# Value sums of the masked keys: from token sums on VectorE and one product with Wv, in place of three products with V

## The chip, the cores and the metric

One core of one Trainium2 chip. The metric is the device time of one execution in microseconds (us), the median of several runs.

## The reference

Eight batches of 512 tokens of width 128. Each token is layer-normalized to `xn`; an attention head and a mixture of 8 experts (the top two of them by gate) both read `xn`, and both results are added to `x`. What matters here is how the attention masks: the scores are multiplied by the mask, so that a masked key has the score 0, and it still takes part in the softmax.

```python
attn = jnp.einsum('bqe,bke->bqk', q, k)
mask = jnp.tril(jnp.ones((T, T), dtype=attn.dtype))
attn = attn * mask
attn = jax.nn.softmax(attn / jnp.sqrt(jnp.asarray(T, attn.dtype)), axis=-1)
return jnp.einsum('bqk,bke->bqe', attn, v)
```

So a row of queries needs, beside the weighted values of the keys it may see, the plain sum of the values of all masked keys, times exp(-max). With T = 512 in NT = 4 tiles of 128 tokens, the keys of all tiles after the query's own are masked for the whole tile; the kernel takes the sum of their values once for each tile of queries.

## The kernel before

All engines run their own lists of instructions, ordered by hand, with semaphores between them. A batch passes through these steps:

- `normal_stats`, `normal_finish` (VectorE), `normal_rstd` (GpSimd), `normalize` (ScalarE) give `xn`; `transpose_x` (TensorE, into a PSUM bank, group X), `x_hi` (ScalarE) and `x_lo` (VectorE) give the transposed tokens as a high and a low part, `xT_hi` and `xT_lo`. A product is three matmuls of these (`three`): high by high, high by low, low by high.
- `wide(b, k, t)` multiplies tile t by a group of the stacked weights: C is Wv, expert 7 and the gates (264 columns), A four experts (512), B three (384). `project_u` (group U) gives `uT` for the scores, with `u_hi` and `u_lo`.
- `c_copy` (ScalarE) copies C, so V too, to SBUF (`c_s`); `scale_experts` (ScalarE) and `mix_b` (VectorE) take A and B out of PSUM; `sum_experts` (GpSimd) adds.
- `scores`, `mask_scores`, `negate_max`, `softmax_exp`, `transpose_probs`, `probs_copy`, `attend` are the attention. The chain for the gates is `gate_max`, `gate_drop`, `gate_below` (VectorE), `gate_exp` (ScalarE), `gate_sum`, `gate_rec`, `gate_out` (VectorE).
- `value_sums` (group SV) multiplies V by a matrix of ones and zeros, `suffix`, one f32 matmul for each of the tiles 1 to 3, so that the rows of query tile t get the sum of the values of all later tiles. `sv_high` (ScalarE) and `sv_rows` (VectorE) put them into the right side of the product `bias`, whose left side comes from `bias_rows` (GpSimd), `transpose_rows` (group DT) and `rows_copy`. `bias` closes the sum in the bank `attb`; `finish_tile` (VectorE) waits for it and writes the output.

The PSUM banks of the groups X, U, SV, DT, A, B and C form a ring of four in a fixed order, and a group waits until the one four places earlier was read. The steady order, for pass n of the loop (n from 1 to 6; + is batch n+1, - is batch n-1), is

```python
GROUPS = "C3 B2- B3- A3- SV DT- A0 B0 X+ A1 B1 C0+ U+ C1+ C2+ A2".split()
...
if prev == "X":
    pe.wait_ge(S["xl_ready"], b + 1)
elif prev in ("U", "SV", "DT"):
    pe.wait_ge(S[{"U": "ul_ready", "SV": "sv_rows_ready", "DT": "dt_ready"}[prev]], b + 1)
```

So U+ waits for what `x_lo` leaves, C2+ for the last `mix_b` of B1 (`mix_ready`), and the next C3 for `u_lo`. TensorE's list has, from C3 on, in pass n: C3(n), B2(n-1), B3(n-1), `attend(n-1, 1)`, `scores(n, 0)`, `transpose_probs(n-1, 2)`, A3(n-1), `transpose_probs(n-1, 3)`, `value_sums(n)`, `attend(n-1, 2)`, `scores(n, 1)`, `transpose_rows(n-1)`, `attend(n-1, 3)`, `bias(n-1)`. VectorE's list, after `x_lo`, has `mask_scores(n-1, 2)`, `mix_b(n-1, 1, 0..2)` with some `normal_stats` between, `u_lo(n)`, `mask_scores(n-1, 3)`, `mix_b(n-1, 2, 0)`, which waits for B2, and then the gates. ScalarE has `softmax_exp(n-1, 3)`, `gate_exp(n)`, `probs_copy(n-1, 2)`, `scale_experts(n-1, 3)`, `probs_copy(n-1, 3)`.

Of the kernel before, what the change touches and what calls it, by code (L numbers as in the profile page):

```python
# [37 lines left out]
ALU = mybir.AluOpType  # L38
# [43 lines left out]
def build(nc, x, w_attention, w_stacked, be, shapes, out):  # L82
# [10 lines left out]
    with ExitStack() as ctx:  # L93
        def sb(name, shape, dt=F32):
            return ctx.enter_context(nc.sbuf_tensor(name, shape, dt))
# [4 lines left out]
        def sem(name):  # L100
# [9 lines left out]
        warm = sb("warm", [P, 1])  # L110
        ident = sb("ident", [P, P])
        causal = sb("causal", [P, NT * P])
        suffix = sb("suffix", [P, NT, P])
        half = sb("half", [P, NT])
        ones = sb("ones", [P, NT, 2, E])

# [38 lines left out]
            veps_ready nmean_ready rstd_ready stats_ready gate_ready nmx_ready tot_ready rinv_ready fin_done  # L155
            rows_ready ffn_ready y7_ready sv_rows_ready stored0 stored_last ones_ready xn0_dve_ready
            wc_ready wcl_ready xt_late_done xh_late_ready rstd0_ready wa_ready wb_ready wla_ready wlb_ready
            ah_ready beh_ready stored1 dve_chain pool_chain ident_ready consts_ready low_ready"""
        S = {n: sem(n) for n in names.split()}

        block = ctx.enter_context(nc.Block())
# [30 lines left out]
        def bank(g, b):  # L192
            return ring[place[g, b] % RING]
# [29 lines left out]
        def _(pe):  # L223
            def ring_free(g, b):

                n = place[g, b] - RING
                if n < 0:
                    return
                prev, b = sequence[n]
                if prev == "X":  # L230
                    pe.wait_ge(S["xl_ready"], b + 1)
                elif prev in ("U", "SV", "DT"):
                    pe.wait_ge(S[{"U": "ul_ready", "SV": "sv_rows_ready", "DT": "dt_ready"}[prev]], b + 1)
                else:
                    pe.wait_ge(S[{"C": "c_used", "A": "a_used", "B": "mix_ready"}[prev[0]]], NT * b + int(prev[1]) + 1)
# [25 lines left out]
            def scores(b, t):  # L261

                if t == 0:
                    pe.wait_ge(S["uh_ready"], b + 1)
                if b * NT + t >= SCORE_BANKS:

                    pe.wait_ge(S["pt_ready"], b * NT + t + 1 - SCORE_BANKS)
                r, n = slice(t * P, (t + 1) * P), (t + 1) * P
                three(score_bank(b, t)[:, 0:n], uT_hi[:, b % 2, r], uT_lo[:, b % 2, r], xT_hi[:, b % 2, 0:n],
                      xT_lo[:, b % 2, 0:n], (S["ul_ready"], b + 1) if t == 0 else None).then_inc(S["scores_done"], 1)  # L270
# [44 lines left out]
            def value_sums(b):  # L315

                ring_free("SV", b)
                pe.wait_ge(S["c_used"], b * NT + NT)
                for m in range(1, NT):
                    last = nc.tensor.matmul(bank("SV", b)[:, 0:P], suffix[:, m, :], c_s[:, b % 2, m, 0:P],  # L320
                                            start=(m == 1), stop=(m == NT - 1))
                last.then_inc(S["sv_done"], 1)

            def transpose_rows(b):

# [132 lines left out]
        def _(dve):  # L458
# [159 lines left out]
            def x_lo(b):  # L618

                dve.wait_ge(S["xh_ready"], b + 1)  # L620
                split_lo(xT_lo[:, b % 2, :], bank("X", b)[:], xT_hi[:, b % 2, :], S["xl_ready"])

            def weights_lo(b):

                dve.wait_ge(S["wa_ready"], 1)
                split_lo(w_lo[:, a_cols], w_f[:, a_cols], w_hi[:, a_cols], S["wla_ready"])
# [28 lines left out]
            dve.wait_ge(S["xh_ready"], 1)  # L655
            split_lo(xT_lo[:, 0, early], bank("X", 0)[:, early], xT_hi[:, 0, early], S["xl_ready"])

            normal_stats(1, 0)
            normal_stats(1, 1)
            normal_stats(1, 2)  # L660
            normal_stats(1, 3)
            bias_rhs(0)
# [17 lines left out]
            mix_b(0, 0, 1)  # L680
            mix_b(0, 0, 2)
            x_lo(1)

            for n in range(1, B - 1):
                mask_scores(n - 1, 2)
                mix_b(n - 1, 1, 0)
                normal_stats(n + 1, 0)
                mix_b(n - 1, 1, 1)
                negate_max(n - 1, 2)
                mix_b(n - 1, 1, 2)  # L690
                normal_stats(n + 1, 1)
                normal_stats(n + 1, 2)
                u_lo(n)
                mask_scores(n - 1, 3)
                mix_b(n - 1, 2, 0)
                negate_max(n - 1, 3)
                mix_b(n - 1, 2, 1)
                normal_stats(n + 1, 3)
                gate_max(n)
                mix_b(n - 1, 3, 0)  # L700
                gate_drop(n)
                gate_below(n)
                softmax_sum(n - 1)
                mix_b(n - 1, 2, 2)
                softmax_tot(n - 1)
                normal_finish(n + 1)
                mix_b(n - 1, 3, 1)
                gate_sum(n)
                mix_b(n - 1, 3, 2)
                mask_scores(n, 0)  # L710
                softmax_rec(n - 1)
                negate_max(n, 0)
                gate_rec(n)
                mask_scores(n, 1)
                negate_max(n, 1)
                finish_tile(n - 1, 0)
                gate_out(n)
                sv_rows(n, 0)
                sv_rows(n, 1)
                sv_rows(n, 2)  # L720
                mix_b(n, 0, 0)
                finish_tile(n - 1, 1)
                mix_b(n, 0, 1)
                finish_tile(n - 1, 2)
                mix_b(n, 0, 2)
                finish_tile(n - 1, 3)
                x_lo(n + 1)

            mix_b(B - 2, 1, 0)
            mix_b(B - 2, 1, 1)  # L730
            mask_scores(B - 2, 2)
            mix_b(B - 2, 1, 2)
            negate_max(B - 2, 2)
# [55 lines left out]
        def _(act):  # L789
# [15 lines left out]
            def c_copy(b, t):  # L805

                act.wait_ge(S["wide_done"], wide_count("C", b, t))
                if t == 0 and b > 1:

                    act.wait_ge(S["pv_done"], (b - 1) * NT)  # L810
                    act.wait_ge(S["sv_done"], b - 1)
                    act.wait_ge(S["y7_ready"], b - 1)
                nc.scalar.copy(c_s[:, b % 2, t, 0:COLS["C"]], bank(f"C{t}", b)[:, 0:COLS["C"]]).then_inc(S["c_used"], 1)

# [165 lines left out]
        def _(pool):  # L980
# [69 lines left out]
            for t in range(1, NT):  # L1050
# [2 lines left out]
            nc.gpsimd.affine_select(out=ident[:], in_=ident[:], compare_op=ALU.not_equal, fill=1.0, base=0,  # L1053
                                    pattern=[[-1, P]], channel_multiplier=1).then_inc(S["ident_ready"], 1)
            nc.gpsimd.memset(top8[:, :, E:E + 2], LOW)
            nc.gpsimd.memset(c_s[:, :, :, COLS["C"]:COLS["C"] + 2], LOW).then_inc(S["low_ready"], 1)
            nc.gpsimd.memset(em[:], 0.0)
            full = chain.mark(nc.gpsimd.memset(causal[:], 1.0))
            cleared = chain.mark(nc.gpsimd.memset(suffix[:], 0.0))
            chain.need(full)  # L1060
            nc.gpsimd.affine_select(out=causal[:, (NT - 1) * P:], in_=causal[:, (NT - 1) * P:], compare_op=ALU.is_ge, fill=0.0, base=0,
                                    pattern=[[-1, P]], channel_multiplier=1)
            chain.need(cleared)

            for m in range(1, NT):
                v = suffix[:, m, :].rearrange("p (t r) -> p t r", r=ROWS)
                last = nc.gpsimd.memset(v[:, 0:m, 0:G_ROW], 1.0)
            chain.step(last)
            normal_rstd(0)
            pool.wait_ge(S["wb_ready"], 1)  # L1070
            nc.gpsimd.tensor_tensor(w_lo[:, b_cols], w_f[:, b_cols], w_hi[:, b_cols].bitcast(F32), ALU.subtract
# [61 lines left out]
```

## Time and profile before

| | |
|---|---|
| median of 3 runs | 132.51 us (130.95 to 132.6) |
| the profiled execution, its own time | 132.71 us |
| its span, from the first to the last instruction | 130.7 us |
| TensorE busy | 121.3 us, 93% |
| VectorE busy | 102.1 us, 78% |
| ScalarE busy | 101.4 us, 78% |
| GpSimd busy | 96.2 us, 74% |

The 1.9 us between the span of the profiled execution and its time lie around the instructions. TensorE's matmuls are pipelined and their ends are modelled, so that its busy time covers short waits too. An instruction on the other engines may start before the record of the one before it has ended. A pass of the steady loop takes 13.90 us.

### The profile page before, as it was taken

The page shows a single profiled execution, that of the slowest core. Times are in us where ns is not written, and L with a number is a line of the kernel's source. Part 1 is how long each engine was busy: PE and PEld are TensorE (multiplying, and loading weights), DVE is VectorE, ACT ScalarE, POOL GpSimd, SP SyncE. Part 2 cuts the span into 40 slices and gives each one's busy share as a digit, 9 for nine tenths or more (in the row PEclk, how much of TensorE's full clock was granted, in tenths as well). Part 3 has the DMA queues.
Part 4 walks back from the last instruction along what each step waited for, and adds up shares of the span by engine and source line. Part 5 has one row for each costly group of instructions (what it writes and reads, how often), then busy time and mean ns, then how long its engine had stood idle before and what let it go on. Part 6 is the DMA issues. An engine that isn't in the chain of part 4 may idle for free.

```text
span 130.7 us, 3014 instructions
## 1 busy us (share of the span) xinstructions
PE 121.3 (93%) x766; PEld 109.1 (83%) x766; DVE 102.1 (78%) x507; ACT 101.4 (78%) x341; POOL 96.2 (74%) x216
## 2 busy tenths in 40 slices
PE   4839999999999999999999999999999999999870
PEld 4717878998989989999899999999899899888650
DVE  0477789797988799697969796979877985967822
ACT  2145699979986999789996999699869999656850
POOL 7080228669995998689967997799859986788881
PEclk9999999999999999999999999999999999999999
DMA  2996000000020002000200020000200020002002
GB/s 65 362 295 164 0 0 8 0 3 3 10 70 5 3 0 80 0 0 3 82 3 3 0 78 10 0 0 7 78 5 0 0 80 0 0 5 83 3 0 80
DMA packets 8929, 5.18 MB, mean 40 GB/s; under 512 B 328, under 2 KB 8784, under 8 KB 8912
## 3 DMA queue, kind: packets, MB, share of 16 engines
q1 hardware_dynamic: 8608, 4.79, 12.5%
q10 hardware_dynamic: 304, 0.20, 0.5%
q8 instruction: 6, 0.10, 0.3%
q14 instruction: 11, 0.09, 0.2%
HBM read 2.89 MB, written 2.10 MB: 38 GB/s over the span
## 4 chain that ended last, share of the span: by engine, by line
PE 83%; DVE 7%; DMA 3%; POOL 2%; ACT 1%; issue 1%; POOLq 0%
PE ring L239 13%; PE ring L240 13%; PE ring L243 13%; PE attb L293 12%; PE score L277 6%; PE ring L320 4%; PE score L243 4%; PE score L240 4%; PE score L239 3%; DMA x_all<-in_x_dram 3%; PE ring L302 2%; PE ring L310 2%; PE ring L313 2%; PE ring L311 2%; DVE xn L648 2%; PE ring L328 1%
## 5 line engine op out<-in xcount | busy, mean ns | idle before, releaser
L829 ACT ACTIVATE ysc<-ring,gate 128x128 f32<-128x128 f32 x128 | 36.4, 372 | 3.4 <-DVE gate L528 1.5
L239 PE MATMUL ring<-w_hi,xT_hi 128*128 128x264 f32 (+2 forms) x96 | 35.2, 367 | 0.6 <-DVE mix L543 0.4
L240 PE MATMUL ring<-w_lo,xT_hi 128*128 128x264 f32 (+2 forms) x96 | 33.0, 344 | 0.0
L243 PE MATMUL ring<-w_hi,xT_lo 128*128 128x264 f32 (+2 forms) x96 | 32.9, 343 | 0.0
L1010 POOL TENSOR_TENSOR ysc<-ysc 128x256 f32<-128x256 f32 x32 | 23.5, 734 | 7.3 <-ACT ysc L829 7.3
L293 PE MATMUL attb<-c_s,probT 128*128 128x128 f32 x160 | 23.3, 278 | 0.0
L543 DVE SCALAR_TENSOR_TENSOR mix<-ring,gate,mix 128x128 f32<-128x128 f32 x64 | 22.0, 344 | 0.2
L239 PEld LDWEIGHTS ring<-w_hi,xT_hi 128*128 128x128 f32 x96 | 18.7, 194 | 3.3 <-DVE mix L543 0.6
L293 PEld LDWEIGHTS attb<-c_s,probT 128*128 128x128 f32 x160 | 20.8, 191 | 0.4
L240 PEld LDWEIGHTS ring<-w_lo,xT_hi 128*128 128x128 f32 x96 | 18.6, 194 | 1.6
L243 PEld LDWEIGHTS ring<-w_hi,xT_lo 128*128 128x128 f32 x96 | 18.5, 193 | 1.4
L1017 POOL TENSOR_TENSOR ffn<-ysc,mix 128x128 f32<-128x128 f32 x32 | 14.6, 457 | 6.5 <-DVE tot L582 4.3
L840 ACT ACTIVATE prob<-score,nmx 128x128 f32<-128x128 f32 (+3 forms) x32 | 17.4, 542 | 0.6 <-DVE nmx L567 0.6
L543 DVE SCALAR_TENSOR_TENSOR mix<-ring,gate,x_all 128x128 f32<-128x128 f32 x32 | 11.0, 345 | 7.9 <-PE ring L243 7.7
L597 DVE SCALAR_TENSOR_TENSOR o_s<-attb,rinv,ffn 128x128 f32<-128x128 f32 x32 | 10.8, 344 | 8.0 <-PE attb L334 7.9
L1013 POOL TENSOR_TENSOR ysc<-ysc,y 128x128 f32<-128x128 f32 x32 | 14.7, 461 | 2.5
L1011 POOL TENSOR_TENSOR ysc<-ysc 128x128 f32<-128x128 f32 x32 | 14.7, 459 | 2.5
L560 DVE CUSTOM_DVE_ANT_0 score<-score,causal 128x128 f32<-128x128 f32 (+3 forms) x32 | 15.7, 490 | 0.1
L990 POOL TENSOR_TENSOR rstd<-veps,half 128x4 f32<-128x4 f32 x8 | 8.1, 1014 | 9.5 <-DVE veps L475 5.9
L277 PE MATMUL score<-ident,prob 128*128 128x128 f32 x80 | 14.2, 276 | 0.2 <-ACT prob L840 0.2
L855 ACT COPY probT<-score 128x128 f32<-128x128 f32 (+3 forms) x32 | 13.8, 430 | 0.4 <-PE score L277 0.3
L801 ACT ACTIVATE xn<-x_all,nmr,rstd 128x128 f32<-128x128 f32 x29 | 12.0, 483 | 1.6 <-POOL nmr L998 1.6
(99 smaller groups left out, 248.9 us busy)
## 6 DMA issues: line engine op xcount, KB each, us to landing
x_all<-in_x_dram SPq DMA_DIRECT2D x8, 256.0 KB, 5.9
out_dram<-o_s SPq DMA_DIRECT2D x7, 256.0 KB, 2.3
w_f<-in_w_stacked_dram SPq DMA_DIRECT2D x1, 580.0 KB, 5.2
out_dram<-o_s SPq DMA_DIRECT2D x1, 192.0 KB, 2.1
wqk_s<-in_w_attention_dram ACTq DMA_DIRECT2D x1, 128.0 KB, 3.7
shapes_s<-in_shapes_dram ACTq DMA_DIRECT2D x1, 64.5 KB
out_dram<-o_s SPq DMA_DIRECT2D x1, 64.0 KB, 1.8
be_s<-in_be_dram ACTq DMA_DIRECT2D x1, 4.0 KB
```

Of the source, the lines that this page charges most:

```text
L239: nc.tensor.matmul(dst, hi, w_h, start=True, stop=False)
L240: nc.tensor.matmul(dst, hi, w_l, start=False, stop=False)
L243: return nc.tensor.matmul(dst, lo, w_h, start=False, stop=True)
L277: last = nc.tensor.transpose(score_bank(b, t)[:, c], prob[:, t, c], ident[:])
L293: last = nc.tensor.matmul(attb[:, t * P:(t + 1) * P], probT[:, b % 2, t, j * P:(j + 1) * P], c_s[:, b % 2, j, 0:P], start=(t == 0), stop=F ...
L543: ins = nc.vector.scalar_tensor_tensor(mix[:, t, i, :], bank(f"B{t}", b)[:, i * P:(i + 1) * P], gate[:, b % 2, t, 4 + i:5 + i], before, AL ...
L560: cnt["maxed", b, t] = chain.mark(nc.vector.tensor_tensor_reduce(score_bank(b, t)[:, 0:n], score_bank(b, t)[:, 0:n], causal[:, (NT - 1 - t ...
L829: last = nc.scalar.mul(ysc[:, t, e, :], bank(f"A{t}", b)[:, e * P:(e + 1) * P], gate[:, b % 2, t, e:e + 1])
L840: nc.scalar.activation(prob[:, t, 0:n], score_bank(b, t)[:, 0:n], ACT.Exp, bias=nmx[:, b % 2, t:t + 1], scale=1.0, accum_out=rs[:, b % 2, ...
L1010: chain.step(nc.gpsimd.tensor_tensor(y[:, 0:2, :], y[:, 0:2, :], y[:, 2:4, :], ALU.add))
L1011: chain.step(nc.gpsimd.tensor_tensor(y[:, 0, :], y[:, 0, :], y[:, 1, :], ALU.add))
L1013: chain.step(nc.gpsimd.tensor_tensor(y[:, 0, :], y[:, 0, :], y7[:, b % 2, t, :], ALU.add))
```

## The change

The sum of the values of a tile's tokens is the sum of its normalized tokens times Wv. VectorE now sums the tokens of tiles 1 to 3 along the free dimension, straight from the PSUM bank of the transposed tokens (`token_sums`, after `x_lo`), adds neighbours (`token_sums_pairs`) and adds the third and spreads the result to the columns of each query tile's rows (`token_sums_later`). One f32 matmul of `x_sums` with the f32 weights (`w_f`, whose first 128 columns are Wv) takes the place of the three. The bank X is now free only once the token sums are taken (`xsum_ready`), and `value_sums` waits for `sums_ready` instead of the copies of V. For batch 0, where tiles 2 and 3 lie in a score bank, there are two reductions, and `scores(0, 2)` waits for them. The constant `suffix` and its memsets go, and two small memsets come.

```diff
@@ ring_free
                 if prev == "X":
-                    pe.wait_ge(S["xl_ready"], b + 1)
+                    pe.wait_ge(S["xsum_ready"], b + 1)
@@ scores
+                if b == 0 and t == 2:
+                    pe.wait_ge(S["xsum_ready"], 1)
@@ value_sums
-                pe.wait_ge(S["c_used"], b * NT + NT)
-                for m in range(1, NT):
-                    last = nc.tensor.matmul(bank("SV", b)[:, 0:P], suffix[:, m, :], c_s[:, b % 2, m, 0:P],
-                                            start=(m == 1), stop=(m == NT - 1))
-                last.then_inc(S["sv_done"], 1)
+                pe.wait_ge(S["sums_ready"], b + 1)
+                if b == 0:
+                    pe.wait_ge(S["w_moe"], 16)
+                nc.tensor.matmul(bank("SV", b)[:, 0:P], x_sums[:].rearrange("p t r -> p (t r)"), w_f[:, 0:P], start=True,
+                                 stop=True).then_inc(S["sv_done"], 1)
@@ new functions on VectorE
+            def token_sums(b):
+                tiles = bank("X", b)[:, P:NT * P].rearrange("p (t k) -> p t k", k=P)
+                nc.vector.tensor_reduce(xs[:, 0:NT - 1], tiles, AX_X, ALU.add).then_inc(S["xsum_ready"], 1)
+            def token_sums_pairs(b):
+                dve.wait_ge(S["xsum_ready"], b + 1)
+                nc.vector.tensor_tensor(xs2[:], xs[:, 0:NT - 1], xs[:, 1:NT], ALU.add).then_inc(S["xs2_ready"], 1)
+            def token_sums_later(b):
+                dve.wait_ge(S["xs2_ready"], b + 1)
+                if b > 0:
+                    dve.wait_ge(S["sv_done"], b)
+                nc.vector.tensor_tensor(x_sums[:, 0:NT - 1, 0:G_ROW], xs2[:].unsqueeze(2).to_broadcast([P, NT - 1, G_ROW]),
+                                        xs[:, 2:NT + 1].unsqueeze(2).to_broadcast([P, NT - 1, G_ROW]), ALU.add
+                                        ).then_inc(S["sums_ready"], 1)
@@ VectorE's list, batch 0
+            dve.wait_ge(S["low_ready"], 1)
+            nc.vector.tensor_reduce(xs[:, 1:NT - 1], late_x[:, early].rearrange("p (t k) -> p t k", k=P), AX_X, ALU.add)
+            nc.vector.tensor_reduce(xs[:, 0:1], bank("X", 0)[:, P:2 * P], AX_X, ALU.add).then_inc(S["xsum_ready"], 1)
             normal_stats(1, 0)
+            token_sums_pairs(0)
             normal_stats(1, 1)
+            token_sums_later(0)
@@ the loop (in the last pass and for batch 1 in the same way)
             for n in range(1, B - 1):
                 mask_scores(n - 1, 2)
+                token_sums_pairs(n)
                 mix_b(n - 1, 1, 0)
                 normal_stats(n + 1, 0)
                 mix_b(n - 1, 1, 1)
+                token_sums_later(n)
                 negate_max(n - 1, 2)
...
                 x_lo(n + 1)
+                token_sums(n + 1)
@@ c_copy on ScalarE
-                    act.wait_ge(S["sv_done"], b - 1)
@@ constants on GpSimd
+            nc.gpsimd.memset(xs[:], 0.0)
+            nc.gpsimd.memset(x_sums[:], 0.0)
...
-            cleared = chain.mark(nc.gpsimd.memset(suffix[:], 0.0))
...
-            for m in range(1, NT):
-                v = suffix[:, m, :].rearrange("p (t r) -> p t r", r=ROWS)
-                last = nc.gpsimd.memset(v[:, 0:m, 0:G_ROW], 1.0)
-            chain.step(last)
```

## Rows read from the trace of the kernel before

**Rows 1.** Windows, one steady pass: PE, PEld, DVE, ACT, POOL busy (count), clock, DMA, GB/s.

```profile
59.30:73.20 13.90, 13.90 (x95) 12.79 (x94) 11.94 (x62) 12.21 (x43) 11.52 (x25) 1.00 0.07 21
```

**Rows 2.** The chain that ended last, 60 to 74 us: start, us, what.

```profile
70.30 0.67 PE ring L320 x6
...
71.99 0.22 PE ring L328
72.22 0.98 PE attb L293 x8
```

**Rows 3.** Timeline of the TensorE weight loads: start, length, [idle before].

```profile
63.58 0.19 PEld L310 LDWEIGHTS ring<-xT_hi,a_hi 128*128 128x128 f32 x1
...
65.35 0.19 PEld L239 LDWEIGHTS ring<-w_hi,xT_hi 128*128 128x128 f32 x1
...
66.29 0.19 PEld L239 LDWEIGHTS ring<-w_hi,xT_hi 128*128 128x128 f32 x1
...
71.89 0.14 PEld L328 LDWEIGHTS ring<-ident,lhs_rows 128*128 128x128 f32 x1
72.04 0.97 PEld L293 LDWEIGHTS attb<-c_s,probT 128*128 128x128 f32 x8
```

**Rows 4.** Timeline of the TensorE matmuls, same pass.

```profile
67.22 0.34 PE L243 MATMUL ring<-w_hi,xT_lo 128*128 128x384 f32 x1
...
72.06 1.15 PE L293 MATMUL attb<-c_s,probT 128*128 128x128 f32 x8
```

**Rows 5.** Timeline of ScalarE, same pass.

```profile
69.87 0.23 ACT L819 ACTIVATE gexp<-below 128x32 f32<-128x32 f32 x1 [1.01 <-DVE below L507]
...
71.38 0.61 ACT L855 COPY probT<-score 128x512 f32<-128x512 f32 x1
```

**Rows 6.** Timeline of GpSimd, same pass.

```profile
71.52 0.26 POOL L1041 TENSOR_TENSOR lhs_rows<-gate_tot,lhs_rows 128x32 fp32r<-128x32 f32 x1
```

**Rows 7.** Timeline of VectorE, same pass.

```profile
62.58 0.68 DVE L480 TENSOR_TENSOR xT_lo<-ring,xT_hi 128x512 fp32r<-128x512 f32 x1
63.18 0.55 DVE L560 CUSTOM_DVE_ANT_0 score<-score,causal 128x384 f32<-128x384 f32 x1
...
64.48 0.35 DVE L543 SCALAR_TENSOR_TENSOR mix<-ring,gate,mix 128x128 f32<-128x128 f32 x1
...
65.23 0.69 DVE L480 TENSOR_TENSOR uT_lo<-ring,uT_hi 128x512 fp32r<-128x512 f32 x1
...
67.60 0.35 DVE L543 SCALAR_TENSOR_TENSOR mix<-ring,gate,x_all 128x128 f32<-128x128 f32 x1 [1.02 <-PE ring L243]
...
69.65 0.19 DVE L507 TENSOR_TENSOR below<-kept,top 128x32 f32<-128x32 f32 x1
...
70.10 0.15 DVE L582 TENSOR_TENSOR tot<-tot,rs 128x4 f32<-128x4 f32 x1
```

**Rows 8.** Timeline of all engines in the last pass.

```profile
113.56 0.26 POOL L1041 TENSOR_TENSOR lhs_rows<-gate_tot,lhs_rows 128x32 fp32r<-128x32 f32 x1
...
113.94 0.14 PEld L328 LDWEIGHTS ring<-ident,lhs_rows 128*128 128x128 f32 x1 [0.24 <-issue]
```

**Rows 9.** Timeline of all engines, start of the kernel.

```profile
15.71 0.91 PE L320 MATMUL ring<-c_s,suffix 128*128 128x128 f32 x6 [0.28 <-ACT c_s L813]
```

**Rows 10.** Groups of instructions by form, whole span.

```profile
L320 PE MATMUL ring<-c_s,suffix 128*128 128x128 f32 x48 | 6.8, 279 | 0.3 <-ACT c_s L813 0.3
...
L480 DVE TENSOR_TENSOR uT_lo<-ring,uT_hi 128x512 fp32r<-128x512 f32 x8 | 5.5, 691 | 1.3 <-ACT uT_hi L859 1.2
...
L560 DVE CUSTOM_DVE_ANT_0 score<-score,causal 128x384 f32<-128x384 f32 x8 | 4.4, 555 | 0.0
...
L513 DVE TENSOR_REDUCE gsum<-gexp 128x4 f32<-128x32 f32 x8 | 1.4, 172 | 0.0
```

**Rows 11.** Timeline of VectorE in the first, shorter pass.

```profile
23.14 0.48 DVE L465 BATCH_NORM_STATS2 stats<-x_all 128x6 f32<-128x128 f32 x2
```

**Rows 12.** Timeline of the weight loads in the first pass.

```profile
24.45 0.19 PEld L239 LDWEIGHTS ring<-w_hi,xT_hi 128*128 128x128 f32 x1 [0.20 <-DVE uT_lo L480]
```

More of the change, by code:

```diff
@@ L112, in build @@
         causal = sb("causal", [P, NT * P])
-        suffix = sb("suffix", [P, NT, P])
+        xs = sb("xs", [P, NT + 1])
+        xs2 = sb("xs2", [P, NT - 1])
+        x_sums = sb("x_sums", [P, NT, ROWS])
         half = sb("half", [P, NT])
@@ L157, in build @@
             wc_ready wcl_ready xt_late_done xh_late_ready rstd0_ready wa_ready wb_ready wla_ready wlb_ready
-            ah_ready beh_ready stored1 dve_chain pool_chain ident_ready consts_ready low_ready"""
+            ah_ready beh_ready xsum_ready xs2_ready sums_ready stored1 dve_chain pool_chain ident_ready consts_ready low_ready"""
         S = {n: sem(n) for n in names.split()}
@@ L682, in _ @@
             x_lo(1)
+            token_sums(1)
             for n in range(1, B - 1):
                 mask_scores(n - 1, 2)
+                token_sums_pairs(n)
                 mix_b(n - 1, 1, 0)
@@ L727, in _ @@
                 x_lo(n + 1)
+                token_sums(n + 1)
             mix_b(B - 2, 1, 0)
+            token_sums_pairs(B - 1)
             mix_b(B - 2, 1, 1)
+            token_sums_later(B - 1)
             mask_scores(B - 2, 2)
@@ L1062, in _ @@
                                     pattern=[[-1, P]], channel_multiplier=1)
-            chain.need(cleared)
-            for m in range(1, NT):
-                v = suffix[:, m, :].rearrange("p (t r) -> p t r", r=ROWS)
-                last = nc.gpsimd.memset(v[:, 0:m, 0:G_ROW], 1.0)
-            chain.step(last)
             normal_rstd(0)
```

## The prediction

> **What bounds the kernel now.** I read the windows first. In a pass of the steady loop TensorE is busy for all of the 13.90 us, at the full clock, with VectorE, ScalarE and GpSimd near 12 us each [rows 1]. That says "TensorE is the bound", and by it every matmul taken away is a gain. But the ends of matmuls are modelled, so I next read the chain that ended last piece by piece. The six records of the three value products take 0.67 us, 0.112 each [rows 2]. The transpose of the rows is one such record and takes 0.22, and the eight records of `attend(n-1, 3)` take 0.98 where 8 x 0.112 is 0.89 [rows 2]. So about 0.2 us of waiting is hidden there. The third view, the timelines, says for what: GpSimd ends the last of the rows at 71.78 and TensorE loads for their transpose at 71.89; ScalarE ends `probs_copy(n-1, 3)` at 71.99 and TensorE loads for `attend(n-1, 3)` at 72.04, and its matmul starts at 72.06 [rows 3 to 6]. TensorE takes both as soon as they are there.
>
> Where do these come from? Backwards on the timelines: `probs_copy(n-1, 3)` lies in ScalarE's unbroken run from `gate_exp`, which starts at 69.87 after 1.01 us of waiting for `gate_below` [rows 5]. `gate_below` ends at 69.84 on VectorE, in an unbroken run that starts at 67.60 with `mix_b(n-1, 2, 0)` after 1.02 us of waiting for B2 [rows 7], whose last matmul ends at 67.22 + 0.34 = 67.56 [rows 4]. GpSimd's part hangs on `softmax_tot`, 70.10, in the same run of VectorE [rows 7]. So from the end of B2 to `attend(n-1, 3)` there is a path of 4.5 us over VectorE and ScalarE (and one over GpSimd) that is as long as what TensorE does meanwhile, waits included. The three value products lie inside this stretch. The rest of the pass, 9.4 us from `attend(n-1, 3)` to the next B2, is TensorE's own work.
>
> **The change part by part.**
>
> *The two products less.* Four of the six records go: 4 x 0.112 = 0.45 us a batch [rows 2], 3.6 us for eight. The remaining one has the same shape (128 x 128, f32), so it keeps 0.22 us. In the steady pass TensorE now comes to the transpose of the rows and to `attend(n-1, 3)` 0.45 us earlier, and both inputs come no earlier, because VectorE's run still starts at the end of B2, ScalarE's with it, and nothing in either is shortened. What TensorE saves it waits. I take 0 for the gain; the bound on the other side is 0.45 less what TensorE waits already, were the two inputs not what it waits for. In the last pass the same rows end on GpSimd at 113.56 + 0.26 = 113.82, and TensorE, which the profile has idle there for 0.24 us, loads at 113.94 [rows 8]: no gain either. At the start the value product waits 0.28 us for the copies of V [rows 9], a wait that goes, but the next work of TensorE there is the transpose of the probabilities, which hangs on VectorE's mask and ScalarE's exponential: 0.
>
> *The reduction.* 384 elements of f32 from PSUM. The trace has no such reduction. The nearest rows are the mask of 384 columns from PSUM, 555 ns, and the reduction of 32 elements, 172 ns; the 512-column split is 691 ns, so an element costs (691 - 555) / 128 = 1.06 ns [rows 10]. 172 + 352 x 1.06 = 545 ns, and the mask's 555 is the other reading. I take 0.55. One instruction starts some 0.08 us before the record ahead of it ends (`x_lo` starts at 62.58, is 0.68 long, and the mask starts at 63.18, [rows 7]), so VectorE's list moves by 0.47 us. From both sides: 0.28 (two elements a step), 1.0 (two steps an element).
>
> *The two small sums.* By `softmax_tot` (0.15) and `gate_below` (0.19) [rows 7], less the overlap of 0.08: 0.07 + 0.11 = 0.18 us. A wait that needs an instruction of its own could double this. Altogether VectorE's list is 0.65 us later from there on, at most 1.2.
>
> *Who waits for that.* VectorE has 1.02 us to spare before `mix_b(n-1, 2, 0)`, so the run of the gates starts as before. Three steps before it are nearer.
> (a) U+ now waits for the reduction instead of `x_lo`. The reduction starts at 63.18 and ends at 63.73; with the 0.05 us from a producer's end to the load (as 71.99 to 72.04, [rows 3, 5]) U loads at 63.78 and not at 63.58 [rows 3]: 0.20 us. Queued behind U are `scores(n, 3)`, C1+, C2+, A2, C3 and B2, all of the path.
> (b) C2+ waits for the third `mix_b` of B1, which ends at 64.48 + 0.35 = 64.83 [rows 7], then at 65.48; its load is at 65.35 [rows 3], or 65.55 after (a): nothing more.
> (c) C3 waits for `u_lo`, 65.23 to 65.92 [rows 7], then to about 66.5; its load is at 66.29 [rows 3], or 66.49 after (a): about nothing more.
> (a), (b) and (c) overlap, so I count one. Loads run ahead of their matmuls, and a few hundredths of a late one are absorbed: 0.17 us for a pass. It lies in the stretch that is TensorE's own work, outside the path over VectorE, so it adds to the pass in full. It happens for batches 2 to 7: 6 x 0.17 = 1.0 us.
> In the first pass VectorE is closer: C3 already waits 0.20 us for `u_lo` there, its load is at 24.45 [rows 12], and VectorE comes to `u_lo` at 23.14 + 0.48 - 0.08 = 23.54 [rows 11]. With 0.65 more it starts at 24.19 and ends at 24.88, and C3 loads at 24.93: 0.45 us (0.48 less the few hundredths).
> Before that, batch 0's reductions go ahead of statistics that have time until `u_lo(0)`: 0, and at most 0.1.
>
> *GpSimd and ScalarE.* The memsets of `suffix` go and two smaller ones come, long before GpSimd's first real work: 0. The wait taken from `c_copy` was on a product long done: 0.
>
> **The sum.** 0 for the products, + 6 x 0.17 + 0.45 = +1.5 us. On the profiled execution's 132.71 us that is 134.2; the median of before is 0.2 lower, so 134.0 us.
>
> [...] The trace shows a reduction of 32 elements no slower than `gate_below` of 32 (172 against about 190 ns, [rows 7, 10]). [...]
>
> **The rivals.**
>
> *TensorE is the bound after all* (the windows are right, and the waits that I read are the model's): 8 x 0.45 = 3.6 us go, and the wait at U costs up to 1.5: 128.9 to 130.4 us. For it: 100% busy, and VectorE's 1.02 us idle. Against it: 0.05 us between ScalarE's end and TensorE's load in the same pass [rows 3, 5], and the rows that take 0.22 instead of 0.11. A half case is that ScalarE's and GpSimd's ends give 0.1 to 0.2 us in a pass: 132.5 to 133.4, within 2%. Chance 0.13 for the full one.
>
> *The reduction is slow.* Of this kernel's mechanisms the one that ends on the other side: U+ waits for it alone, and every 0.1 us over 0.55 adds 0.1 in each of seven batches, 0.7 us in all. The time is above 135.2 (2%) when it takes over about 0.70 us; at 1.0 us it is 134.0 + 7 x 0.45 = 137.2. By then VectorE is also 1.1 us later and uses up its 1.02 us before B2. For it: unseen size and PSUM source, two added waits; in the first pass there is no slack at all. Against it: every row of VectorE from PSUM shows one element in 1.06 ns. Chance 0.17, mostly at 135.3 to 136.5.
>
> *The change doesn't do what it says*: if the one product with `w_f` took as long as the three, nothing in my sum would change, since I count no gain. It has no case of its own.
>
> **How the numbers follow.** My forecast, 132.3 to 135.2, has 0.70: two hundredths of a us in (a) are 0.1 us in the time, and the half case of the first rival lies in it. Faster by over 2% is below 129.9: 0.12. Slower by over 2%: 0.18. 2% is about what a measurement of this kernel tells from no change (its three runs of before lie 1.2% apart). The range leaves out the full first rival and the far end of the second: 131.2 to 136.0.
>
> **What would show each step.** The value product as two records of about 0.11 us in place of six. The reduction near 0.55 us, right after `x_lo`. TensorE's load for U some 0.05 us behind the reduction's end, with the wait put down to VectorE. TensorE waiting 0.4 to 0.6 us in a pass before the transpose of the rows or `attend(n-1, 2)` and `attend(n-1, 3)`, for ScalarE and GpSimd. VectorE's wait for B2 down from 1.02 to about 0.5 us. A steady pass of 14.05 to 14.1 us. I am wrong if the pass is 13.6 or less (the path over VectorE is not what TensorE meets), or if U doesn't wait.

## The result, and the profile after

The changed kernel takes 135.88 us (median of 4 runs) where the kernel before takes 132.56 beside it: a ratio of 1.0257, 95% interval 1.0195 to 1.0319. So it is slower, and whether by more than 2% the interval leaves just open. The profiled execution took 136.31 us, its span is 134.3, 3.6 us more than before. One kernel below, the window form in the first new order, had two slow executions in ten, its profiled one among them; ratios leave such executions out.

The page of the changed kernel, parts 1 and 2 (share of the span by engine, TensorE, and the granted clock in tenths):

```profile
PE 121.8 (91%) x734; PEld 106.2 (79%) x734; DVE 107.9 (80%) x532; ACT 101.9 (76%) x341; POOL 95.9 (71%) x214
...
PEclk9975799999999999999999999999999999999999
```

TensorE is busy for 121.8 us, as before (121.3 in the table above), though 32 records of value products are gone; VectorE went from 102.1 to 107.9. The clock row tells of the start: in the changed kernel's profiled execution the granted clock is 0.50 until about 15.2 us, and the 264-column matmuls take 0.42 us up to there. In the profile of the kernel before, the clock row says full speed all along, but the same matmuls take 0.42 us there too, and 0.28 from about 14.7 on. By these lengths TensorE got faster some 0.5 us later in the changed kernel. With it the first mask on VectorE starts at 15.76 instead of 15.47: 0.29 us that are not the change's, since TensorE's work up to there is the same. The kernels below differ among themselves at the start in the same way, with the token sums or without (14.72 to 15.97 for the first mask), so I compare passes. A pass is the distance between the starts of two `bias` matmuls:

```profile
60.82 0.48 PE L338 MATMUL attb<-rhs_rows,lhsT_rows 128*128 128x512 f32 x1
...
75.22 0.48 PE L338 MATMUL attb<-rhs_rows,lhsT_rows 128*128 128x512 f32 x1
```

| start of `bias` to the next, us | n=2 | 3 | 4 | 5 | 6 | last |
|---|---|---|---|---|---|---|
| before | 13.91 | 13.91 | 13.90 | 13.90 | 13.93 | 14.13 |
| changed | 14.40 | 14.42 | 14.40 | 14.39 | 14.48 | 14.43 |

The labels n are the passes of the loop in which the second of the two `bias` matmuls stands; pass 6 is a case of its own, told with the third experiment. Six passes give 2.8 us, the stretch from the first mask to the first `bias` (15.47 to 31.24 before, 15.76 to 32.00 after) 0.47, and the start 0.29: the 3.6 us. Where in a pass? The chain that ended last, 60 to 76 us (start, us, what), has two pieces of the stretch between `attend` and B2 that are longer than their neighbours of the same size:

```profile
65.64 0.40 PE ring L314
66.04 0.24 PE ring L315
...
67.57 0.04 issue
67.61 0.39 PE ring L241
68.00 0.12 PE ring L242
```

The first matmul of U takes 0.40 where the next takes 0.24, and the first of C2 takes 0.39, with 0.04 of issue ahead, where the next takes 0.12: 0.16 and 0.31 us, together nearly the whole of the 0.50. The weight loads and VectorE's list of the same pass, which answer to [rows 3, 7], say who is late:

```profile
65.54 0.19 PEld L314 LDWEIGHTS ring<-xT_hi,a_hi 128*128 128x128 f32 x1
...
67.61 0.19 PEld L241 LDWEIGHTS ring<-w_hi,xT_hi 128*128 128x128 f32 x1 [0.25 <-DVE mix L547]
...
72.29 0.30 PEld L325 LDWEIGHTS ring<-w_f,x_sums 128*128 128x128 f32 x2
72.78 0.74 PEld L297 LDWEIGHTS attb<-c_s,probT 128*128 128x128 f32 x6 [0.19 <-ACT probT L888]
...
74.15 0.14 PEld L332 LDWEIGHTS ring<-ident,lhs_rows 128*128 128x128 f32 x1 [0.28 <-issue]
```

```profile
64.34 0.69 DVE L484 TENSOR_TENSOR xT_lo<-ring,xT_hi 128x512 fp32r<-128x512 f32 x1
64.94 0.55 DVE L630 TENSOR_REDUCE xs<-ring 128x3 f32<-128x384 f32 x1
...
65.88 0.16 DVE L635 TENSOR_TENSOR xs<-xs 128x3 f32<-128x3 f32 x1
...
66.66 0.57 DVE L642 TENSOR_TENSOR x_sums<-xs 128x9 f32<-128x9 f32 x1
...
67.22 0.34 DVE L547 SCALAR_TENSOR_TENSOR mix<-ring,gate,mix 128x128 f32<-128x128 f32 x1
...
69.86 0.35 DVE L547 SCALAR_TENSOR_TENSOR mix<-ring,gate,x_all 128x128 f32<-128x128 f32 x1 [0.66 <-PE ring L245]
```

U loads at 65.54, behind the reduction, which ends at 64.94 + 0.55 = 65.49: the wait that was foretold, with the length that was foretold. C2 loads at 67.61, 0.05 us behind the third `mix_b` of B1 (67.22 + 0.34 = 67.56). That `mix_b` is late because of an instruction of nine elements, `token_sums_later`, that took 0.57 us. It took as long in batches 2 to 5 (0.57 to 0.59), 0.15 or 0.16 in batches 0, 1 and 6, and 0.35 in the last:

```profile
L642 DVE TENSOR_TENSOR x_sums<-xs x8: 150/461/595, 12.3 to 109.5; 128x9 f32<-128x9 f32 x8
```

The numbers after the count are minimum, median and maximum in ns. GpSimd's list at that time:

```profile
66.47 0.74 POOL L1043 TENSOR_TENSOR ysc<-ysc 128x256 f32<-128x256 f32 x1
67.29 0.46 POOL L1044 TENSOR_TENSOR ysc<-ysc 128x128 f32<-128x128 f32 x1
67.82 0.46 POOL L1046 TENSOR_TENSOR ysc<-ysc,y 128x128 f32<-128x128 f32 x1
```

The small sum starts at 66.66, while GpSimd adds 128x256 in SBUF, and ends at 67.23, 0.02 us behind the end of GpSimd's instruction (66.47 + 0.74 = 67.21). All seven long instances of the two small sums in this trace end 0.01 to 0.03 us behind an instruction of GpSimd. A large one with only one operand in SBUF is not held: `u_lo`, out of PSUM and SBUF, starts inside GpSimd's instruction of 67.82 and takes its usual time (0.67; 0.69 in the kernel before):

```profile
67.87 0.67 DVE L484 TENSOR_TENSOR uT_lo<-ring,uT_hi 128x512 fp32r<-128x512 f32 x1
```

And in the other stretch TensorE waits for what it saved: after the one product (72.29, two loads) it is idle for 0.19 us before `attend(n-1, 2)`, for ScalarE's copy of the probabilities, and for 0.28 us before the transpose of the rows (74.15).

### The profile page after: what moved, and what is told of

Same layout as the page of the kernel before. It is cut to its first block, busy times and chain, and to the rows that moved or that the text cites. A ratio compares the mean times of both kernels' runs of the same rounds, so it can differ in the third digit from the quotient of the medians.

```text
span 134.3 us, 2973 instructions
## 1 busy us (share of the span) xinstructions
PE 121.8 (91%) x734; PEld 106.2 (79%) x734; DVE 107.9 (80%) x532; ACT 101.9 (76%) x341; POOL 95.9 (71%) x214
## 4 chain that ended last, share of the span: by engine, by line
PE 47%; DVE 16%; issue 4%; ACT 3%; POOL 2%; POOLq 0%; DVEq 0%
PE attb L297 10%; PE ring L241 8%; PE ring L245 7%; PE ring L242 7%; DVE mix L547 5%; PE score L281 4%; DVE rhs_rows L612 2%; DVE o_s L601 2%; PE score L242 2%; PE score L245 2%; PE score L241 2%; DVE xT_lo L484 1%; PE ring L332 1%; ACT ysc L862 1%; PE ring L306 1%
## 5 line engine op out<-in xcount | busy, mean ns | idle before, releaser
L241 PE MATMUL ring<-w_hi,xT_hi 128*128 128x264 f32 (+2 forms) x96 | 36.0, 375 | 0.9 <-DVE mix L547 0.4
L297 PE MATMUL attb<-c_s,probT 128*128 128x128 f32 x160 | 23.9, 282 | 0.3 <-ACT probT L888 0.3
L547 DVE SCALAR_TENSOR_TENSOR mix<-ring,gate,mix 128x128 f32<-128x128 f32 x64 | 21.9, 342 | 0.2
L1050 POOL TENSOR_TENSOR ffn<-ysc,mix 128x128 f32<-128x128 f32 x32 | 14.7, 458 | 6.4 <-DVE tot L586 4.3
L1044 POOL TENSOR_TENSOR ysc<-ysc 128x128 f32<-128x128 f32 x32 | 14.7, 460 | 2.5
L1046 POOL TENSOR_TENSOR ysc<-ysc,y 128x128 f32<-128x128 f32 x32 | 14.7, 460 | 2.5
L547 DVE SCALAR_TENSOR_TENSOR mix<-ring,gate,x_all 128x128 f32<-128x128 f32 x32 | 11.1, 345 | 6.0 <-PE ring L245 5.8
```

Source lines behind the costliest of these rows:

```text
L241: nc.tensor.matmul(dst, hi, w_h, start=True, stop=False)
L297: last = nc.tensor.matmul(attb[:, t * P:(t + 1) * P], probT[:, b % 2, t, j * P:(j + 1) * P], c_s[:, b % 2, j, 0:P], start=(t == 0), stop=F ...
L547: ins = nc.vector.scalar_tensor_tensor(mix[:, t, i, :], bank(f"B{t}", b)[:, i * P:(i + 1) * P], gate[:, b % 2, t, 4 + i:5 + i], before, AL ...
L1044: chain.step(nc.gpsimd.tensor_tensor(y[:, 0, :], y[:, 0, :], y[:, 1, :], ALU.add))
L1046: chain.step(nc.gpsimd.tensor_tensor(y[:, 0, :], y[:, 0, :], y7[:, b % 2, t, :], ALU.add))
```

## The experiments

Two theories. The path theory is the prediction's: the saving of the product is worth nothing, since TensorE meets a path from B2 over VectorE, ScalarE and GpSimd; the loss is the wait at U and, as the profile after adds, the held small sum. Its rival: TensorE is the bound, the saving is real, and the token sums cost some 7 us.

**The product alone.** Edit, against the changed kernel:

```diff
-                    pe.wait_ge(S["xsum_ready"], b + 1)
+                    pe.wait_ge(S["xl_ready"], b + 1)
...
-                pe.wait_ge(S["sums_ready"], b + 1)
...
-                token_sums_pairs(n)
-                token_sums_later(n)
-                token_sums(n + 1)
```

> The one product alone: one f32 matmul in place of three, and no token sums at all (x_sums stays zero, so the value sums of the masked keys are left out); the bank of X is freed by x_lo as before. The path theory (from the end of B2 over VectorE, ScalarE and GpSimd to attend is what TensorE meets): TensorE waits for what it saves, the pass stays at 13.85 to 13.90 us, the time at 132.3 to 132.6. The rival (TensorE is the bound): 0.45 us less in each of 8 batches, pass 13.45, time 129.0.

Measured: 132.54 us, ratio to before 1.0037 (0.9999 to 1.0074), pass 13.91 us. Two of three products are gone in all eight batches, nothing was put in their place, and the pass didn't move. The weight loads of one pass show where the 0.45 us went:

```profile
69.96 0.30 PEld L323 LDWEIGHTS ring<-w_f,x_sums 128*128 128x128 f32 x2
70.48 0.74 PEld L295 LDWEIGHTS attb<-c_s,probT 128*128 128x128 f32 x6 [0.22 <-ACT probT L876]
...
71.84 0.14 PEld L330 LDWEIGHTS ring<-ident,lhs_rows 128*128 128x128 f32 x1 [0.28 <-issue]
72.00 0.97 PEld L295 LDWEIGHTS attb<-c_s,probT 128*128 128x128 f32 x8
```

0.22 us of waiting for ScalarE before `attend(n-1, 2)` and 0.28 before the transpose of the rows, neither of which the kernel before has. For the second the profile names nobody ("issue"); GpSimd ends the last of the rows at 71.73, 0.11 us before the load, the same distance as in the kernel before (71.78 and 71.89). The rival's 129.0 us is out.

**The token sums alone.** Edit, against the changed kernel:

```diff
-                nc.tensor.matmul(bank("SV", b)[:, 0:P], x_sums[:].rearrange("p t r -> p (t r)"), w_f[:, 0:P], start=True,
-                                 stop=True).then_inc(S["sv_done"], 1)
+                pe.wait_ge(S["c_used"], b * NT + NT)
+                for m in range(1, NT):
+                    last = nc.tensor.matmul(bank("SV", b)[:, 0:P], suffix[:, m, :], c_s[:, b % 2, m, 0:P],
+                                            start=(m == 1), stop=(m == NT - 1))
+                last.then_inc(S["sv_done"], 1)
```

> The token sums alone: the changed kernel with the three value products on V kept, the sums from the tokens taken and waited for but not used. The path theory: the saving of the product was worth nothing, so keeping the three products costs nothing against the changed kernel: pass 14.40 us, time 135.7 to 136.1. The rival: 0.45 us more a batch than the changed kernel, pass 14.85, time 139.5.

Measured: ratio 1.0301 (1.0237 to 1.0365), 135.79 us, pass 14.42. Against the changed kernel's 135.88 us: with 0.45 us more of TensorE's work in each batch the time is the same to within 0.1 us. With the first run this splits the result: the whole loss is the sums', the gain of the product is nil.

**The small sum at a later place.** Edit, in the loop and alike in the last pass:

```diff
                 mix_b(n - 1, 1, 1)
-                token_sums_later(n)
...
                 mask_scores(n - 1, 3)
+                token_sums_later(n)
                 mix_b(n - 1, 2, 0)
```

> The changed kernel with the second small sum (token_sums_later, 0.57 us long in batches 2 to 5) moved from between two mix_b of B1 to just before the mix_b that waits for B2, where VectorE has 0.66 us to spare. If the long small sum is what makes C2 wait for mix_b, the wait at C2 goes and the wait at U (0.17) stays: pass 14.1, time 134.0 to 134.4. Rival (the delay comes from the reduction, and C2 waits for it anyway): the pass stays at 14.3 or more, time 135.5.

Measured: ratio 1.0226 (1.0164 to 1.0288), 134.72 us, passes of 14.09, 14.08, 14.09, 14.09 and then 14.51 and 14.30. The pass fell as the path theory has it; the time is 0.3 us above what was expected. The profiled execution alone, 135.61 us, is 0.9 us later than the changed kernel's by the first `bias` (32.91 against 32.00): its granted clock is 0.50 until about 19.7 us, and a 384-column matmul takes 0.52 us there in place of 0.34. What the median keeps is the pass of 14.51, pass 6. There the other small sum, `token_sums_pairs`, is held (0.36 us), but that makes C2 only 0.09 us late. The larger part is at its start: VectorE stands for 0.21 us ahead of `sv_rows`, for nothing that the profile names, and X waits for `sv_rows`:

```profile
90.44 1.05 DVE L612 SCALAR_TENSOR_TENSOR rhs_rows<-sv_hi,shapes_s,ring 3x128 fp32r<-3x128 f32 x3 [0.21 <-issue]
...
94.62 0.36 DVE L635 TENSOR_TENSOR xs<-xs 128x3 f32<-128x3 f32 x1
...
97.59 0.16 DVE L642 TENSOR_TENSOR x_sums<-xs 128x9 f32<-128x9 f32 x1
```

```profile
91.55 0.42 PEld L306 LDWEIGHTS ring<-ident,xn 128*128 128x128 f32 x4 [0.39 <-DVE rhs_rows L612]
```

The changed kernel and the one with the token sums alone have the same stop of 0.21 us at the same place of pass 6, and X waits 0.37 and 0.38 us. The kernel before, the product alone and the window form below have not. So about 0.3 us of the changed kernel's loss has a cause that no run here shows.

**One small sum with one operand from SBUF.** Edit:

```diff
-                nc.vector.tensor_tensor(xs2[:], xs[:, 0:NT - 1], xs[:, 1:NT], ALU.add).then_inc(S["xs2_ready"], 1)
...
-                nc.vector.tensor_tensor(x_sums[:, 0:NT - 1, 0:G_ROW], xs2[:].unsqueeze(2).to_broadcast([P, NT - 1, G_ROW]),
-                                        xs[:, 2:NT + 1].unsqueeze(2).to_broadcast([P, NT - 1, G_ROW]), ALU.add
-                                        ).then_inc(S["sums_ready"], 1)
+                flat = xs[:, 0:NT - 1]
+                windows = bass.AP(flat.tensor, flat.offset, [list(flat.ap[0]), [1, NT - 1], [0, G_ROW], [1, NT - 1]])
+                nc.vector.tensor_reduce(x_sums[:, 0:NT - 1, 0:G_ROW], windows, AX_X, ALU.add
+                                        ).then_inc(S["sums_ready"], 1)
```

> The changed kernel with the two small sums, of which each reads two operands from SBUF, replaced by one reduction over overlapping windows of three, with one operand from SBUF, in the place of the second. If the small sum is long because of its two SBUF operands while GpSimd reads SBUF (it ends with GpSimd's instruction, 67.21 and 67.23 in the trace): the reduction is 0.17 us long in every batch, C2 waits no more than 0.05 us, pass 14.1, time 134.0. Rival (the length comes from the place or from the wait for a semaphore): it is 0.5 us or longer there as well, and the time stays at 135.5 or more.

Measured: ratio 1.0183 (1.0132 to 1.0235), 134.28 us, pass 14.08. All eight of the reductions are short, the one of this pass beside the same instruction of GpSimd that held the sum before:

```profile
L644 DVE TENSOR_REDUCE x_sums<-xs x8: 164/173/176, 12.1 to 107.8; 128x9 f32<-128x27 f32 x8
```

```profile
66.03 0.17 DVE L644 TENSOR_REDUCE x_sums<-xs 128x9 f32<-128x27 f32 x1
```

```profile
65.92 0.74 POOL L1041 TENSOR_TENSOR ysc<-ysc 128x256 f32<-128x256 f32 x1
```

It starts at 66.03 and ends at 66.20, in the midst of GpSimd's 65.92 to 66.66. So neither the place nor the semaphore makes the sum long (in batches 1 and 6 of the changed kernel the sum itself was short at that place and behind that semaphore); two operands from SBUF beside GpSimd do (0.57 to 0.59 us in four batches of the changed kernel, against 0.164 to 0.176 with one). That it is the two operands and not the kind of instruction rests on `u_lo` above, a `tensor_tensor` with one operand in SBUF; no run has a small one. The pass is the one predicted (14.05 to 14.1), pass 6 included, with the wait at U as its only cost.

**Tokens summed out of SBUF.** Edit, on top of the window sum (batches 1 to 7; both steps go to where VectorE waits for B2, and `x_hi` waits for the sums of two batches before):

```diff
-                    pe.wait_ge(S["xsum_ready"], b + 1)
+                    pe.wait_ge(S["xsum_ready" if b == 0 else "xl_ready"], b + 1)
...
-                tiles = bank("X", b)[:, P:NT * P].rearrange("p (t k) -> p t k", k=P)
+                tiles = xT_hi[:, b % 2, P:NT * P].bitcast(F32).rearrange("p (t k) -> p t k", k=P)
...
                 u_lo(n)
+                token_sums(n)
                 mask_scores(n - 1, 3)
+                token_sums_later(n)
                 mix_b(n - 1, 2, 0)
```

> The window form, but the tokens of batches 1 to 7 are summed from xT_hi in SBUF, between u_lo and mask_scores(n-1, 3), where VectorE has time before B2, and the window sum just before the mix_b that waits for B2. So U+ waits for x_lo alone, as before the change. Left out: the low parts of the tokens in the sums. Path theory: the wait at U was the last 0.17 us of a pass, and the product still gives nothing: pass 13.90 to 13.95, time 132.5 to 132.8. Rival (part of the 0.17 is TensorE's own): the pass stays at 14.05 or more, time 134. Or, were TensorE the bound, the saving would now show: 129.5.

Measured: ratio 0.9948 (0.9899 to 0.9997), 131.9 us, pass 13.91. The first matmul of U is back at 0.23 us in the chain: the wait at U was the last of the cost. The time is below the 132.5 to 132.8 expected. VectorE's wait for B2 went from 1.02 us [rows 7] to what is left of it beside both sums:

```profile
65.92 0.54 DVE L630 TENSOR_REDUCE xs<-xT_hi 128x3 f32<-128x384 f32 x1
...
66.98 0.17 DVE L644 TENSOR_REDUCE x_sums<-xs 128x9 f32<-128x27 f32 x1
67.70 0.35 DVE L547 SCALAR_TENSOR_TENSOR mix<-ring,gate,x_all 128x128 f32<-128x128 f32 x1 [0.55 <-PE ring L245]
```

With all costs gone, the pass is that of before: once more the product gives nothing.

**The path made shorter.** Edit in the loop, ScalarE's list and VectorE's:

```diff
                 softmax_exp(n - 1, 3)
-                gate_exp(n)
                 probs_copy(n - 1, 2)
-                scale_experts(n - 1, 3)
+                gate_exp(n)
                 probs_copy(n - 1, 3)
+                scale_experts(n - 1, 3)
...
                 gate_max(n)
+                mix_b(n - 1, 2, 2)
                 mix_b(n - 1, 3, 0)
+                softmax_sum(n - 1)
                 gate_drop(n)
-                gate_below(n)
-                softmax_sum(n - 1)
-                mix_b(n - 1, 2, 2)
                 softmax_tot(n - 1)
+                gate_below(n)
```

On the kernel before:

> The kernel before with the path made shorter by order alone, in the loop: ScalarE copies probs(n-1, 2) ahead of gate_exp and probs(n-1, 3) ahead of scale_experts; VectorE does mix_b(n-1, 2, 2) and softmax_sum ahead of gate_drop and softmax_tot ahead of gate_below. Path theory: TensorE's own work with three products is 13.8 us, so only its 0.1 us of waiting goes: pass 13.78 to 13.85, time 131.7 to 132.2. Rival (the order is what bounds, at large): pass 13.5 or less, time 130.

Measured: ratio 0.9911 (0.9877 to 0.9945), 131.63 us, pass 13.85. With one product and no sums:

> The one product without token sums (value sums left out), as in the run of the product alone, with the same new order of the loop. Path theory: now TensorE is the bound and the 0.45 us of a pass come out: pass 13.35 to 13.45, six passes, time 129.3 to 129.9. Rival (something else waits at the same place, or the product's saving isn't real): pass 13.8 or more, time 132.

Measured: ratio 0.9932 (0.9902 to 0.9961), 131.79 us, pass 13.84. The expectation failed: with this order too, two products less give nothing. On the window form:

> The window form of the changed kernel (134.3, pass 14.08) with the same new order of the loop. Path theory: the wait at U stays (0.17), the product's 0.45 and the 0.1 of waiting come out: pass 13.55 to 13.65, time 131.3 to 131.9. Rival (VectorE, with 0.55 us more work a pass, is the bound as soon as the path is shorter): pass 13.8 or more, time 132.7 or more.

Measured: ratio 1.0016 (0.9985 to 1.0048), 133.24 us for all ten executions and 132.89 for the eight in the ratio, pass 14.03 where 13.6 was expected. In the profiled execution a 384-column matmul takes 0.52 us until about 20.5 us, and its usual 0.34 in the steady passes. What took the path's place shows in the run with one product. Its weight loads, VectorE and GpSimd:

```profile
74.17 0.42 PEld L304 LDWEIGHTS ring<-ident,xn 128*128 128x128 f32 x4 [0.37 <-DVE rhs_rows L610]
```

```profile
72.42 0.35 DVE L599 SCALAR_TENSOR_TENSOR o_s<-attb,rinv,ffn 128x128 f32<-128x128 f32 x1 [0.33 <-PE attb L336]
72.69 0.46 DVE L530 TENSOR_TENSOR gate<-gexp,grec 128x32 f32<-128x32 f32 x1
73.08 1.04 DVE L610 SCALAR_TENSOR_TENSOR rhs_rows<-sv_hi,shapes_s,ring 3x128 fp32r<-3x128 f32 x3
```

```profile
72.64 0.47 POOL L1032 TENSOR_TENSOR ysc<-ysc 128x128 f32<-128x128 f32 x1
```

`bias` now comes earlier, and VectorE's `gate_out` behind it, with two operands from SBUF, falls into a GpSimd instruction (72.64 to 73.11) and takes 0.46 instead of 0.18. So `sv_rows` is late, and X waits for it, 0.37 us, which the kernel before did not. X waits 0.36 us in the window form too. The one pass in which it wasn't held, the first, took 13.54.

**A second order.** Edit, on top of the first:

```diff
                 negate_max(n, 1)
-                finish_tile(n - 1, 0)
                 gate_out(n)
                 sv_rows(n, 0)
                 sv_rows(n, 1)
                 sv_rows(n, 2)
+                finish_tile(n - 1, 0)
```

> The one product without token sums (value sums left out), with a second order: the first one, and in the loop VectorE does gate_out ahead of the wait for bias and the three sv_rows right behind it, before finish_tile(n-1, 0). In the run with the first order X now waited 0.38 us for sv_rows, because gate_out (two operands from SBUF) took 0.46 us beside GpSimd. Path theory: with that path 0.65 us shorter TensorE is the bound at last: pass 13.40 to 13.50, time 129.3 to 130.0. Rival (the saving is lost at yet another place, or isn't there): pass 13.75 or more, 131.5.

> The kernel before, three products, with the second order. Path theory: TensorE's own work is the bound, 0.45 us over the run with one product: pass 13.80 to 13.86, time 131.5. Rival (it is the order that gains, not the product): the same pass as with one product.

Measured: one product 130.57 us, ratio 0.985 (0.9781 to 0.9919), pass 13.56; three products 130.85, ratio 0.988 (0.982 to 0.9941), pass 13.72. The product is worth 0.16 us in a pass, not 0.45. Expected were 13.40 to 13.50 with one product and 13.80 to 13.86 with three; that of one is longer, that of three shorter. The two times, 0.28 us apart with overlapping intervals, don't tell the two kernels apart; the passes do. The chain of the kernel with three products (start, us, what):

```profile
70.53 0.11 PE ring L328
70.64 0.89 PE attb L293 x8
71.53 0.24 PE attb L334
```

No piece is longer than its work: here TensorE is the bound, at 13.72 us a pass, so that the kernel before had 0.18 us of waiting in its 13.90, as its chain said [rows 2]. With one product:

```profile
70.72 0.24 PE ring L330
70.96 0.89 PE attb L295 x8
71.86 0.42 PE attb L336
```

0.13 us of waiting before the transpose of the rows, whose input GpSimd ends at 70.51, and 0.18 before `bias`, whose input ScalarE copies until 71.66:

```profile
70.26 0.25 POOL L1062 TENSOR_TENSOR lhs_rows<-gate_tot,lhs_rows 128x32 fp32r<-128x32 f32 x1
```

```profile
71.35 0.31 ACT L907 CAST lhsT_rows<-ring 128x128 fp32r<-128x128 f32 x1
```

0.16 + 0.13 + 0.18 = 0.47: the 0.45 us are all accounted for, and two thirds of them still wait, now for `bias_rows` and `rows_copy`.

The new order has a cost of its own, in the same way as the small sum. `softmax_tot` now stands ahead of `gate_below` and lets GpSimd go on just before it, and `gate_below`, with two operands from SBUF, is held by what GpSimd does:

```profile
69.04 0.15 DVE L584 TENSOR_TENSOR tot<-tot,rs 128x4 f32<-128x4 f32 x1
69.15 0.41 DVE L509 TENSOR_TENSOR below<-kept,top 128x32 f32<-128x32 f32 x1
```

```profile
69.06 0.45 POOL L1038 TENSOR_TENSOR ffn<-ysc,mix 128x128 f32<-128x128 f32 x1
```

It takes 0.40 or 0.41 us in five batches of every kernel in a new order, and 0.19 in the kernel before [rows 7]. ScalarE's list runs without a stop from `gate_exp`, which waits for it, to the `rows_copy` that `bias` waits for. So the 0.22 us are on that path. That without them `bias` would wait no more is an estimate from 0.22 against 0.18; no run shows it. The other two kernels in this order:

> The window form of the changed kernel, exact, with the second order. Path theory: the wait at U is the only cost left and it adds: pass 13.60 to 13.70, time 130.5 to 131.2. Rival (VectorE's list, 0.55 us longer, now bounds): pass 13.9 or more, time 132.5.

Measured: 131.98 us, ratio 0.9955 (0.9924 to 0.9986), pass 13.75: 0.19 over the run with one product alone, which is the wait at U (the first matmul of U takes 0.42 in the chain and 0.24 there). Both are above what was expected, by 0.05 in the pass and 0.8 in the time.

> Token sums of batches 1 to 7 from xT_hi in SBUF (low parts left out), window sum, second order. Path theory: neither the wait at U nor the long path: pass 13.45 to 13.55, time 129.5 to 130.3, the best of all. Rival: VectorE is late for B2's mix_b, since the reduction, the window sum and GpSimd's sharing eat the 1.0 us it has: pass 13.7 or more.

Measured: 130.29 us, ratio 0.9824 (0.9763 to 0.9884), pass 13.56. It is the fastest, but its interval overlaps that of the three products in the same order, 130.85, whose pass is 0.16 longer. Both beat the kernel before and the changed one.

## Why the prediction was right or wrong

The direction was right, the size wasn't: 134.0 us were forecast, a loss of 1.5, and 135.88 measured, a loss of 3.3. The forecast with the chance of 0.70, 132.3 to 135.2, missed the time; the part above 135.2 had 0.18. The wide range, 131.2 to 136.0, held it by 0.12 us, and by luck: its upper end was set for a slow reduction, and the reduction wasn't slow.

- *What bounds the kernel, and the gain of 0.* Right, and shown: with the product alone the pass stayed at 13.91 us, and with or without it the sums gave the same time. TensorE met the inputs of `attend(n-1, 2)` and of the transpose of the rows, and waited 0.19 + 0.28 = 0.47 us for them where 0.4 to 0.6 was foretold. The wait of about 0.2 us read from the chain was 0.18, by the pass of 13.72 in which there is none.
- *The reduction.* 0.55 us estimated, 0.55 measured (548 to 552 ns in all seven batches that have it); a mask of as many elements takes 0.555 us [rows 10]. The two sides that I gave it, 0.28 and 1.0 us, were my estimates of about half and about twice that; no run shows either. The second rival, a slow reduction, didn't happen, though the time came out on its side.
- *(a), the wait at U.* Right: 0.17 foretold, 0.16 measured; with the reduction and the window sum moved the pass fell by it (14.08 to 13.91).
- *The first stretch.* 0.45 foretold, 0.47 measured, but not by the step foretold alone. C2 waits there too, 0.32 us for the third `mix_b` (its load at 24.11, [0.32 <-DVE mix L547]). C3's load follows `u_lo` by 0.05 us as foretold, at 25.09; that is 0.35 us more than before when the 0.29 of the start are taken off, not 0.48, and the rest comes after it. The closeness of the size is in part luck.
- *The two small sums, and with them (b), C2 "nothing more".* This is the step that failed. I priced them at 0.18 us by the rows of `softmax_tot` and `gate_below` [rows 7] and let them at most double. The doubling was my estimate for the waits, and it didn't show: `token_sums_later` stands behind two waits and still starts 0.09 us before the record ahead of it ends (66.66 against 66.41 + 0.34 = 66.75). In four of the six passes `token_sums_later` alone took 0.57 or more. The third `mix_b` of B1 then ended 3.22 us after the start of `x_lo` (64.34 to 67.56), where my sum has 2.90 (62.58 to 65.48): 0.32 later than I had it, and C2 waited 0.31. The window form, in which no sum is held, gave 14.08, inside the foretold 14.05 to 14.1. The warning was in the trace of before, in a view that I read for means only: the instances of one small sum of two SBUF operands there range from 153 to 419 ns, those of `gate_out` from 178 to 455:

```profile
L577 DVE TENSOR_TENSOR tot<-em,masked_keys x8: 153/160/419, 28.0 to 123.4; 128x4 f32<-128x4 f32 x8
L528 DVE TENSOR_TENSOR gate<-gexp,grec x8: 178/182/455, 18.6 to 115.7; 128x32 f32<-128x32 f32 x8
```

A minimum and a maximum a factor of 2.5 apart are a price too.
- *What my forecast is short of, 1.9 us, is not all of it the small sums.* The window form takes 1.6 us less (134.28), and 0.3 of these are the wait of X in pass 6, whose cause is open. In the profiled execution 0.29 us more come from the later start; what they make in the median can't be said.
- *The rival that TensorE is the bound* is refuted by the first two runs.

That the 0.45 us would come out once the path was shorter was a belief of the experiments, not of the prediction. Of the two orders tried only the second gave any of it back, a third.

## What to carry to other kernels

Take the busiest engine's work away only after you have found, at the next few places where it takes something from another engine, how long that lay ready; here it was 0.05 us, and 0.45 us of work a pass became 0.45 us of waiting. When an instruction is added to an engine that is not the bound, look for the spread of its like in the trace, not for its mean, and ask what GpSimd does at that moment: seven of the sixteen small sums here ended with an instruction of GpSimd, at 0.34 to 0.59 us in place of 0.15 or 0.16. And try whether the result can be had from one operand: the reduction over windows in place of the two sums took 0.164 to 0.176 us in all eight batches.

## What the hardware showed that I had not expected

In these traces small VectorE instructions with two operands from SBUF (the two small sums, `below`, `tot`, `gate`) end with the GpSimd instruction that they start inside: where they start 0.04 us or more behind its start and it has 0.30 us or more to go, they end 0.01 to 0.07 us behind its end, in all 128 instances of the fourteen traces. `softmax_tot`, where it starts together with a GpSimd instruction (0.00 or 0.01 us behind), takes its 0.15 us. Nine elements took 0.15 us alone and 0.57 to 0.59 in four batches of the changed kernel; the one shown ends 0.02 us behind GpSimd's. A reduction of 27 elements with one SBUF operand took 0.164 to 0.176 us in all eight batches, five of them starting 0.10 or 0.11 us inside a GpSimd instruction of 0.74 or 0.75 us. In all the long ones GpSimd came first; that a GpSimd instruction is held in its turn by VectorE, these readings do not show.
